# A four-layer transformer kernel: two attentions reordered, one with its softmax division moved behind the value products

## The reference, cut to what matters

```python
# third attention (L2): 32 query heads in 8 groups; a group shares one key and one value head; head size 128
q, k = rope(x @ Wq), rope(ctx @ Wk); v = ctx @ Wv
scores = where(mask, q k^T / sqrt(128), -1e9); out = (softmax(scores) @ v) @ Wo
# last attention (L3): 16 heads of 4 states x 8 columns
qh, kh, vh = interfere(proj(x)), interfere(proj(ctx)), interfere(proj(ctx))
scores = einsum('bhqdm,bhkdm->bhqkm', qh, kh) / sqrt(8)
weights = softmax(scores, axis=keys)         # per head and state
out = einsum('bhqkm,bhkdm->bhqdm', weights, vh) @ Wo.T + bo
```

## Time and profile before

| | |
|---|---|
| median of the runs, us | 1784.14 (1775.97 to 1784.38) |
| profiled execution, us | 1782.34, span 1781.0 |
| TensorE products / weight loads busy | 1626.8 us, 91% / 1170.5 us, 66% |
| VectorE, ScalarE, GpSimd busy | 1007.3 us, 57% / 500.6 us, 28% / 578.0 us, 32% |
| chain that ended last | TensorE 75%, VectorE 13%, ScalarE 5%, GpSimd 3%, issue 3% |
| mean granted clock of TensorE | 0.963 |

### The profile page before, as it was taken

One profiled execution on the slowest core, in us unless ns is written; L12 is line 12 of the kernel. 1 busy time (PEld: TensorE's weight loads), 2 busy tenths in 40 slices (PEclk: granted clock), 3 DMA queues, 4 the chain that ended last, 5 costly groups with the idle time before them and its releaser, 6 DMA issues.

```text
span 1781.0 us, 21304 instructions
## 1 busy us (share of the span) xinstructions
PE 1626.8 (91%) x8900; PEld 1170.5 (66%) x8900; DVE 1007.3 (57%) x1328; ACT 500.6 (28%) x744; POOL 578.0 (32%) x377
## 2 busy tenths in 40 slices
PE   8889989998899989999999999998899876879998
PEld 2264358886468768777787787877664454548887
DVE  6987862224715555455564545644551688466665
ACT  4130020002431133243232332322112477630000
POOL 4917732220543313133131332311040244651221
PEclk9989999999999989999999999998899999889999
DMA  3000041003000130101011010100301021400000
GB/s 120 1 1 1 1 166 47 24 0 124 13 0 1 40 112 26 36 24 38 22 60 36 24 36 24 36 1 1 144 0 24 1 49 26 182 0 7 13 13 18
DMA packets 18016, 66.49 MB, mean 37 GB/s; under 512 B 1440, under 2 KB 9760, under 8 KB 13312
## 3 DMA queue, kind: packets, MB, share of 16 engines
q1 hardware_dynamic: 17920, 65.12, 10.5%
HBM read 58.82 MB, written 2.10 MB: 34 GB/s over the span
## 4 chain that ended last, share of the span: by engine, by line
PE 75%; DVE 13%; ACT 5%; POOL 3%; issue 3%; DMA 1%; SPq 0%; DVEq 0%; ACTq 0%; POOLq 0%
PE banks L270 45%; PE banks L264 24%; PE banks L399 2%; DVE arena L442 1%; PE banks L1870 1%; DVE arena L234 1%; DVE arena L1411 1%; POOL w_lo L2333 1%; ACT dense L1978 1%; PE banks L2132 1%; POOL arena L1577 1%; DVE grouped_split L1443 1%; PE banks L1275 1%; ACT dense L1990 1%; ACT arena L1511 1%
## 5 line engine op out<-in xcount | busy, mean ns | idle before, releaser
L270 PE MATMUL banks<-grouped_split 128*128 128x512 f32 x1536 | 384.4, 405 | 12.4 <-DVE grouped_split L1443 6.2
L270 PEld LDWEIGHTS banks<-grouped_split 128*128 128x128 f32 x1536 | 291.4, 194 | 80.8 <-DVE grouped_split L1443 9.4
L1577 POOL TENSOR_TENSOR arena<-arena,grouped 128x512 f32<-128x512 f32 x80 | 102.7, 1288 | 350.4 <-ACT arena L1511 350.3
L270 PE MATMUL banks<-experts_split 128*128 128x512 f32 (+1 forms) x792 | 180.1, 389 | 1.9 <-DVE experts_split L627 1.9
L270 PEld LDWEIGHTS banks<-experts_split 128*128 128x128 f32 (+1 forms) x792 | 146.1, 185 | 35.2 <-DVE experts_split L624 2.1
L1398 DVE TENSOR_TENSOR arena<-banks,grouped 128x512 f32<-128x512 f32 x80 | 54.7, 684 | 153.0 <-ACT arena L1511 153.0
L264 PE MATMUL banks<-arena 128*128 128x64 f32 (+2 forms) x730 | 123.0, 324 | 14.0 <-DMA arena<-in_c 6.5
L264 PEld LDWEIGHTS banks<-arena 128*128 128x128 f32 x730 | 107.4, 204 | 36.4 <-issue 27.0
L655 DVE SCALAR_TENSOR_TENSOR arena<-banks,experts,arena 128x512 f32<-128x512 f32 x64 | 47.8, 751 | 111.3 <-PE banks L270 111.3
L264 PE MATMUL banks<-dense 128*32 128x64 f32 (+4 forms) x1738 | 86.1, 294 | 23.9 <-ACT dense L1978 9.2
L1411 DVE TENSOR_TENSOR arena<-arena 128x512 f32<-128x512 f32 x80 | 70.7, 883 | 58.8 <-POOL arena L1577 58.7
(11 more groups left out here) (288 smaller groups left out, 3030.4 us busy)
## 6 DMA issues: line engine op xcount, KB each, us to landing
grouped<-in_attn SPq DMA_DIRECT2D x16, 1024.0 KB, 5.0
experts<-in_expert SPq DMA_DIRECT2D x8, 1024.0 KB, 4.9
linear<-in_ffn SPq DMA_DIRECT2D x1, 4096.0 KB, 15.0
grouped<-in_attn SPq DMA_DIRECT2D x8, 512.0 KB, 3.6
dense<-arena SPq DMA_DIRECT2D x16, 256.0 KB, 4.9
dense<-in_w SPq DMA_DIRECT2D x1, 3584.0 KB, 12.2
dense<-in_attn SPq DMA_DIRECT2D x1, 3072.0 KB, 12.7
dense<-in_w SPq DMA_DIRECT2D x1, 2688.0 KB, 10.1
```

The costliest lines, as they stand in the source:

```text
L270: s = pe.matmul(dst, lhsT=lhsT[i], rhs=rhs[j], start=(k == 0 and x == 0), stop=(k == n - 1 and x == 2))
L1577: g_.tensor_tensor(rot, rot, f(SIN + h * HALF, HALF), ALU.mult).then_inc(rot_sin.sem, 1)
```

## The change

In `attn2`, TensorE issues head 2 before the second half's transposes, then `k_rows` of the second half, then `apply`, head 3 and the outputs; `group_uses()` and the other engines' rotary calls follow that order, VectorE splitting the keys' rotary work around `apply_low`. The next group's first queries wait for head 3's rotary sum.

In `attn3`, the transposes take the exponentials undivided. `times_v` also multiplies a block `ONE` (32 columns for each half, set once) with the same transposed data, which puts the sums into the other half of bank 6; VectorE takes their reciprocal and multiplies, writing the result where `keep` wrote it. `total`, the divisions and `keep` go; `values` moves from ScalarE to GpSimd. TensorE's iteration j is score(j+2), turn(j), key rows, times_v(j), and the key projections run one unit further ahead. In `ffn3`, ScalarE waits for the last value products and, before its third copy, for the last result.

```diff
@@ -1130,8 +1130,8 @@
-        uses += [("q", g + 1, 1, 0), ("q", g + 1, 2, 0)] * nxt + [("a", g, 1, j) for j in range(4)]
-        uses += [("q", g + 1, 3, 0), ("k", g + 1, 1, 0)] * nxt + [("o", g, t, 1) for t in range(4)]
+        uses += [("q", g + 1, 1, 0), ("q", g + 1, 2, 0), ("k", g + 1, 1, 0)] * nxt + [("a", g, 1, j) for j in range(4)]
+        uses += [("q", g + 1, 3, 0)] * nxt + [("o", g, t, 1) for t in range(4)]
@@ -1322,7 +1322,7 @@
-                pe.wait_ge(*rot_add(at_turn["k", g, 1, 0] + 1))
+                pe.wait_ge(*rot_add(at_turn["q", g, 3, 0] + 1))
...
             q_rows(g, 0, 1, lambda c: score(0, c))
@@ -1357,13 +1357,13 @@
                 q_rows(g + 1, 1, 0)
+                q_rows(g + 1, 2, 0)
             turn(g, 1)
...
-                q_rows(g + 1, 2, 0)
+                k_rows(g + 1, 1)
             apply(g, 1)
...
                 q_rows(g + 1, 3, 0)
-                k_rows(g + 1, 1)
@@ -1479,10 +1479,11 @@
+                rotary_cos(("k", g + 1, 1, 0))
             apply_low(g, 1)
...
+                rotary_add(("k", g + 1, 1, 0))
...
-                rotary(("k", g + 1, 1, 0))
@@ -1560,14 +1561,14 @@
+                rotary(("q", g + 1, 2, 0))
             turn(g, 1)
...
-                rotary(("q", g + 1, 2, 0))
+                rotary(("k", g + 1, 1, 0))
...
-                rotary(("k", g + 1, 1, 0))
...
     def pool(g_):
         def rotary(u):
@@ -1601,9 +1602,10 @@
-                for q in range(1, QH2):
-                    rotary(("q", g + 1, q, 0))
+                rotary(("q", g + 1, 1, 0))
+                rotary(("q", g + 1, 2, 0))
...
+                rotary(("q", g + 1, 3, 0))
...
+    ONE, INV = W0 + 768, R + 10880
@@ -1861,7 +1864,7 @@
         def turn(j, h):
-            pe.wait_ge(*att_done(2 * j + h // 2 + 1))
+            pe.wait_ge(*exp_done(j + 1))
@@ -1875,6 +1878,8 @@
+            pe.wait_ge(*zero_set(3))
+            pe.wait_ge(*one_set(1))
@@ -1884,8 +1889,13 @@
+                            mm(pe, bank[32 * h:32 * h + 32, 6, (2 * p + b2) * S:(2 * p + b2 + 1) * S],
+                               f(VX + (b * 2 + a) * P + 32 * h, 32), f(PT + (h * 4 + p * 2 + a) * P + b2 * S, S), a, 2)
+            for p in range(2):
+                for a in range(2):
+                    for h in range(4):
+                        s = mm(pe, bank[32 * h:32 * h + 32, 6, 256 + p * P:256 + (p + 1) * P], f(ONE + 32 * a, 32),
+                               f(PT + (h * 4 + p * 2 + a) * P, P), a, 2)
@@ -1897,27 +1907,24 @@
-            T, u = j // UN, j % UN
             if j + 2 < NU:
                 score(j + 2)
-            if j:
-                for h in range(4):
-                    turn(j - 1, h)
-            else:
+            if j == 0:
...
                 q_rows(7)
-            if T + 1 < DC:
-                if u % 2 == 0:
-                    n = 2 * (T + 1) + u // 2
+            for h in range(4):
+                turn(j, h)
+            n = (j + 5) // 2
+            if n < 2 * DC:
+                if j == 0:
+                    pe.wait_ge(*q_out(8))
+                    k_rows(1, 0, 7, range(DC))
+                elif j % 2:
                     pe.wait_ge(*k_out(n))
-                    if n == 2:
-                        pe.wait_ge(*q_out(8))
-                k_rows(T + 1, u // 2, 7, range(2 * (u % 2), 2 * (u % 2) + 2))
-            if j:
-                times_v(j - 1)
-        for h in range(4):
-            turn(NU - 1, h)
-        times_v(NU - 1)
+                    k_rows(n // 2, n % 2, 7, range(2))
+                else:
+                    k_rows(n // 2, n % 2, 7, range(2, DC))
+            times_v(j)
...
     def vector(v):
@@ -1940,19 +1947,21 @@
-        def total(j):
-            pr, tot = f(PR[j], 2048, 32, S), f(W0 + 800, 32)
-            v.wait_ge(*exp_done(j + 1))
+        def divide(j):
+            T, u = j // UN, j % UN
+            v.wait_ge(*o_mm(j + 1))
+            v.reciprocal(f(INV, 256), bank[:, 6, 256:512]).then_inc(inv_done.sem, 1)
+            v.wait_ge(*inv_done(j + 1))
+            v.tensor_tensor(f(OT + T * N + u * 256, 256), bank[:, 6, 0:256], f(INV, 256), ALU.mult).then_inc(ot_done.sem, 1)
+
+        top(0)
+        top(1)
+        for j in range(NU):
             if j:
-                v.wait_ge(*att_done(2 * j))
-            m.own(v, v.tensor_reduce(tot, pr, axis=AX, op=ALU.add))
-            v.reciprocal(tot, tot).then_inc(sum_done.sem, 1)
-
-        top(0)
-        for j in range(NU):
-            if j + 1 < NU:
-                top(j + 1)
-            total(j)
+                divide(j - 1)
+            if j + 2 < NU:
+                top(j + 2)
+        divide(NU - 1)
...
     def scalar(act):
@@ -1979,19 +1988,6 @@
-        def values(T, h):
...
         def exps(j):
@@ -2004,11 +2000,6 @@
-        def keep(j):
-            T, u = j // UN, j % UN
-            act.wait_ge(*o_mm(j + 1))
-            act.activation(f(OT + T * N + u * 256, 256), bank[:, 6, 0:256], ACT.Copy).then_inc(ot_done.sem, 1)
-
@@ -2019,28 +2010,23 @@
+        act.wait_ge(*zero_set(1))
+        for k in range(M3):
+            s = act.activation(f(ONE + k // 2 * 32 + k * 8, 8), m.const("m_half")[:, 2 * (k % 2):2 * (k % 2) + 1].broadcast_to(
+                [P, 8]), ACT.Copy)
+        s.then_inc(one_set.sem, 1)
...
-            T, u = j // UN, j % UN
...
-            if j >= 2:
-                keep(j - 2)
-            if u == 0:
-                values(T, 0)
-            if u == 2:
-                values(T, 1)
-            if j:
-                turned(j - 1)
-            if T + 1 < DC and u % 2:
-                keys(T + 1, u // 2)
-        keep(NU - 2)
-        turned(NU - 1)
-        keep(NU - 1)
+            turned(j)
+            if j % 2 == 0 and j // 2 + 2 < 2 * DC:
+                keys((j // 2 + 2) // 2, j // 2 % 2)
 
     def pool(g):
+        g.memset(f(ONE, 64), 0.0).then_inc(zero_set.sem, 1)
@@ -2048,11 +2034,20 @@
-        for j in range(NU):
-            g.wait_ge(*sum_done(j + 1))
-            for h in range(2):
-                pr, tot = f(PR[j] + h * 1024, 1024, 16, S), f(W0 + 800 + 16 * h, 16)
-                g.tensor_tensor(pr, pr, tot.unsqueeze(2).broadcast_to([P, 16, S]), ALU.mult).then_inc(att_done.sem, 1)
+
+        def values(T, h):
+
+            g.wait_ge(*vd_in(64 * (T + 1)))
+            if T:
+                g.wait_ge(*o_mm(UN * (T - 1) + 2 * h + 2))
+            for k in range(M3):
+                s = g.tensor_scalar(vx[:, 8 * h:8 * h + 8, k // 2, :, k, :].rearrange("p b h d -> p b h d"),
+                                    f(VD + h * 1024, 1024).rearrange("p (b h m d) -> p b h m d", b=8, h=4, m=M3)[:, :, :, k, :],
+                                    m.const("m_half")[:, 2 * (k % 2):2 * (k % 2) + 1], None, ALU.mult)
+            s.then_inc(vx_done.sem, 1)
+
+        for n in range(2 * DC):
+            values(n // 2, n % 2)
@@ -2279,7 +2274,10 @@
+        act.wait_ge(*m.o_mm(16))
...
+            if c == 2:
+                act.wait_ge(*m.ot_done(16))
...
```

More of the change, by code:

```diff
@@ L1762, in attn3 @@
         m.sem(f"attn3_{n}") for n in ("zero", "vx", "score_mm", "score_read", "exp"))
-    sum_done, att_done, turn_mm, turn_out, o_mm, ot_done = (
-        m.sem(f"attn3_{n}") for n in ("sum", "att", "turn_mm", "turn_out", "o_mm", "ot"))
+    one_set, inv_done, turn_mm, turn_out, o_mm, ot_done = (
+        m.sem(f"attn3_{n}") for n in ("one", "inv", "turn_mm", "turn_out", "o_mm", "ot"))
     m.c1_in = m.sem("ffn3_c1_in")
@@ L1886, in times_v @@
                         for h in range(4):
-                            s = mm(pe, bank[32 * h:32 * h + 32, 6, (2 * p + b2) * S:(2 * p + b2 + 1) * S],
-                                   f(VX + (b * 2 + a) * P + 32 * h, 32), f(PT + (h * 4 + p * 2 + a) * P + b2 * S, S), a, 2)
+                            mm(pe, bank[32 * h:32 * h + 32, 6, (2 * p + b2) * S:(2 * p + b2 + 1) * S],
[5 more added lines that the diff above has]
+                               f(PT + (h * 4 + p * 2 + a) * P, P), a, 2)
             s.then_inc(o_mm.sem, 1)
@@ L1980, in keys @@
             s.then_inc(k_out.sem, 1)
-        def values(T, h):
-            act.wait_ge(*vd_in(64 * (T + 1)))
-            if T:
-                act.wait_ge(*o_mm(UN * (T - 1) + 2 * h + 2))
-            else:
-                act.wait_ge(*zero_set(2))
-            for k in range(M3):
-                s = act.activation(vx[:, 8 * h:8 * h + 8, k // 2, :, k, :].rearrange("p b h d -> p b h d"),
-                                   f(VD + h * 1024, 1024).rearrange("p (b h m d) -> p b h m d", b=8, h=4, m=M3)[:, :, :, k, :],
-                                   ACT.Copy, scale=m.const("m_half")[:, 2 * (k % 2):2 * (k % 2) + 1])
-            s.then_inc(vx_done.sem, 1)
         def exps(j):
```

## The result

| | before | changed |
|---|---|---|
| median, us (runs) | 1780.62 (4) | 1753.62 (4) |
| range of the runs, us | 1775.97 to 1784.38 | 1748.2 to 1756.28 |
| span of the profiled execution, us | 1781.0 | 1755.0 |
| mean granted clock | 0.963 | 0.967 |

A forecast was written before the change was run, and what follows sets the result against it. The prediction took TensorE with its waits to bound the third attention, and a ring across engines, not TensorE, the last. It summed 1782.3 - 7.0 - 1.5 - 10.7 = 1763.1 us, range 1756 to 1774.

The forecast's parts named there:

- the wait of 1.17 us: Third attention, TensorE within the value products, waiting for VectorE's first rotary product of head 2: forecast to go.
- one of 0.71 stays (0.72): Third attention, TensorE ahead of head 3, behind the keys' rotary work and first low part: 0.72 us forecast to remain.
- The seams between kinds of products: Third attention: the moved key rows lose 0.5 us, 0.2 given back, so 1.0 us saved a group instead of 1.3.
- slow heads: Third attention, head 3 at 4.60 us instead of 3.05 in two groups: 3.1 us in all, 1.5 forecast saved.
- the walk through the loop: Last attention, unit-by-unit timing of TensorE's chain to the end of the last products: 10.7 us saved, 5 to 13.
- The rival by serial ones: Last attention: 32 passes of 128 columns run one behind another, 4.1 us instead of 1.03, kernel 1803 us; chance 0.05.
- odd-to-even steps: Last attention, from an odd unit's value products to the next even unit's, carried by TensorE: 7.4 us.
- even-to-odd step: Last attention, from an even unit's value products to the next odd unit's, set by ScalarE's masks and exponential: 8.2 us.
- The last step: Last attention, from unit 14's value products to those of unit 15, which has no scores: 5.3 us.
- the move to GpSimd: Last attention, value scaling on GpSimd, 3 us a half: costs nothing, up to 3 us once.
- more than forecast: Whole kernel: slow heads go entirely (1.5), reordering reaches 2.1 more and the loop 2.3, or most: 1757 to 1759; chance 0.13.

The follow-up runs named there:

- e4_head2_only: The kernel before, with the second query head moved ahead of the transposes but the key rows left behind the third head: 1769.34 us, ratio 0.9938.
- e5_ones_twice: The changed kernel with each of the 16 products with the ones issued twice into the same columns: 1755.14 us, ratio 0.9867.
- e7_one_mask_on_vector: The changed kernel with the fourth of four key masks of each half on VectorE instead of ScalarE: 1749.28 us, ratio 0.9826.
- e10_short_reciprocal: The changed kernel with the reciprocal over 8 columns instead of 256, most of the division left out: 1751.54 us, ratio 0.9835.
- e2_joined_only: The kernel before with only the changes in attn3 and ffn3, the third attention in its old order: 1768.1 us, ratio 0.9930.

## Why the prediction missed, step by step

- **Right:** the wait of 1.17 us goes, one of 0.71 stays (0.72). **Wrong in the size:** "The seams between kinds of products take some back ... I take 1.0 us a group". The group lost 1.37, and the stalls 2.03 - 0.71 = 1.32. The step that failed is the 0.3 taken off for seams. The key rows do take 3.53 now, but their old place cost the same elsewhere: behind them the 51 products of the earlier trace rows, the outputs', took 12.14 us, and now head 3 and they together, 63, take 14.59: 12 more for 2.45, where a head by itself takes 3. 2.6 us of the miss.
- **Wrong:** of the slow heads' 3.1 us "the stall that precedes them shrinks but one stays, so I take half". None is left, nor in `e4_head2_only`, where 1.65 us of waits a group stay. That a head falls to the lower clock is not in proportion to the wait ahead of it. 1.6 us of the miss.
- **Right:** the walk through the loop. Its steps were 8.09 and 7.16 (8.2 and 7.4), its length 119.5 us (120.2); the saving 11.4 (10.7), which is 0.7 of the miss. The rival by serial ones is out, as they take 1.06 us; `e5_ones_twice` shows that in the pairs they count on odd-to-even steps. ScalarE carries the even-to-odd step (`e7_one_mask_on_vector`), as the walk had it. The last step, 6.75 for 5.3, fell to the lower clock (0.57 from 1506 to 1510); without that it is 5.14, in `e10_short_reciprocal`.
- **Right:** nothing for the move to GpSimd. The first two halves' 8 operations take 7.25 us from 1396.91, so the first half is there at about 1400.5, and the first value products, at 1402.65, wait for no GpSimd. The Trainium skill ("GPSIMD Engine Reference", "Instruction dispatch") has the first call of a freshly loaded routine pay about 6 us. The trace shows no such time: the first operation starts where the memsets end, at 1396.91, and all take 0.91. Whether the routine had to be loaded, no run shows.
- **Not forecast:** the rest. With the right sizes the sum is 1782.3 - 9.6 - 3.1 - 11.4 = 1758.2, inside the range. The execution of before that the sum stood on was 1.7 us above the median that the changed kernel was compared with. That leaves 2.9 us, of which the traces show 1.4 behind the loop; there all other traces are shorter than that of before too (238.6 to 240.4, for 241.8), whatever was changed, so it was the execution of before that was long. The last 1.5 are not placed. The changed kernel's profiled execution, 1756.28, was the slowest of its four, 2.7 above their median.

The rival "more than forecast" (1757 to 1759, chance 0.13) was thus right in mechanism for the third attention, where both its terms came, while the loop gained 0.7 of its 2.3. Even its lower end was 3 us high: the range ended 1 us under it, with hardly any room for the variation of a measurement.

## What to carry to other kernels

On a bound engine the stalls that went were worth their full length here. Before taking something off for the place that work moves to, look in the rows for what its old place costs. A loop in which three engines have steps of 7 to 8 us is worth a walk by units, and a trade between engines in it can come back on the next engine: 0.67 us off ScalarE's step came to 0.07 a unit. And put the difference between executions of unchanged code into the range's ends.

## What the runs showed of the hardware

- The same code up to the first transposes of `attn2` took between 684.9 and 693.9 us over the 14 traces: 9 us, as much as one part of this change brings.
- The loop of before ran between granted clocks of 0.87 and 0.97 in three traces (1400 to 1515), the joined one at 0.99 in the changed kernel, 0.97 in `e2_joined_only` and 1.00 in `e5_ones_twice`, with TensorE 98.7, 101.2 and 105.0 us busy for 82.6 to 85.1. The two ranges meet at 0.97; no run tells the order's part in this from how full TensorE is.
- Under a load at 395 to 452 GB/s TensorE stopped for 2 us without a wait in two kernels, and in `e5_ones_twice` for 1.5 at another place (358 GB/s); in the changed kernel's three traces the same load stopped nothing.
- The reciprocal out of PSUM took 1.76 us for 256 columns, a product of 256 columns 0.42: 4.2 times as much.
